# A windowed attention stage: strips issued ahead of stores, its end joined to the next stage, its first two groups' queries set in the stage in front

## What is computed

```python
x = x + 0.5 * _L0_ffn_ref(_layernorm(x, axis=-1), ...)
x = x + _L0_attn_ref(_layernorm(x, axis=-1), ...)
x = x + 0.5 * _L0_ffn_ref(_layernorm(x, axis=-1), ...)
x = x + 0.5 * _L1_ffn_ref(_layernorm(x, axis=-1), ...)
x = x + _L1_attn_ref(_layernorm(x, axis=-1), ...)
x = x + 0.5 * _L1_ffn_ref(_layernorm(x, axis=-1), ...)
```

```python
qkv = (x @ Wqkv.T + bqkv).reshape(B, S, 3, H, d).transpose(2, 0, 3, 1, 4)
...
scores = jnp.einsum('bhncd,bhnld->bhncl', qc, kb) / np.sqrt(d)
...
scores = jnp.where(band, scores, -jnp.inf)
attn = jax.nn.softmax(scores, axis=-1)
o = jnp.einsum('bhncl,bhnld->bhncd', attn, vb).reshape(B, H, S, d)
...
return o @ Wout.T + bout
```

## Time and profile before

| | us |
|---|---|
| median of 3 runs | 1857.52 |
| lowest and highest | 1851.13, 1860.44 |
| the profiled execution | 1860.59 |
| its span, first to last instruction | 1858.4 |

### The profile page before, as it was taken

The page is one execution under the profiler, slowest core; times in us unless marked ns, Lnnn a source line. Parts: engine busy times, 40 slices in busy tenths (PEclk is TensorE's granted clock), DMA queues, the critical chain, the costliest instruction groups (busy, mean ns, idle before and its releaser), DMA issues. The chain is left out here.

```text
span 1858.4 us, 40266 instructions
## 1 busy us (share of the span) xinstructions
PE 1652.9 (89%) x14217; PEld 1417.0 (76%) x14217; DVE 1260.3 (68%) x2948; ACT 1073.2 (58%) x1947; POOL 1196.9 (64%) x1189
## 2 busy tenths in 40 slices
PE   7999898998999989987788999999888788889999
PEld 6888777787878868766567888788767677777887
DVE  2359889888798887988996436443457677646443
ACT  3476766766667766666664544343467566643442
POOL 4238787886878758788896706465655555434663
PEclk9999999999999989999999999999888898889999
DMA  5023333233333323232231501111555556311113
GB/s 151 1 72 117 96 103 111 95 97 98 106 90 120 102 79 110 82 113 87 81 97 29 154 6 48 35 48 43 156 164 148 158 153 177 86 33 38 48 48 106
DMA packets 141088, 171.22 MB, mean 92 GB/s; under 512 B 32246, under 2 KB 76316, under 8 KB 140892
## 3 DMA queue, kind: packets, MB, share of 16 engines
q1 hardware_dynamic: 133852, 153.06, 27.6%
q0 software_dynamic: 7040, 15.60, 2.7%
HBM read 116.30 MB, written 52.30 MB: 91 GB/s over the span
## 5 line engine op out<-in xcount | busy, mean ns | idle before, releaser
L833 POOL TENSOR_TENSOR db<-du_m,bt 128x512 f32<-128x512 f32 x256 | 328.4, 1284 | 115.3 <-DVE bank L838 114.6
L838 DVE TENSOR_TENSOR_SCAN bank<-bank,db 128x512 f32<-128x512 f32 x256 | 312.6, 1221 | 18.3 <-ACT bank L823 17.8
L864 POOL TENSOR_TENSOR y_m<-y_m,ph 128x512 f32<-128x512 f32 x240 | 313.1, 1305 | 2.0 <-DVE ph L853 2.0
L823 ACT ACTIVATE bank<-dt_m,a_neg 128x512 f32<-128x512 f32 x256 | 176.3, 689 | 88.2 <-DVE ph L853 81.2
L853 DVE TENSOR_TENSOR ph<-bank,ct 128x512 f32<-128x512 f32 x240 | 165.9, 691 | 8.4
L1368 POOL TENSOR_TENSOR s_a<-s_a,mx_a 128x768 f32<-128x768 f32 x64 | 94.1, 1471 | 74.4 <-DVE mx_a L1459 73.4
L1445 PE MATMUL bank<-kT_a,qd_a 128*128 128x96 f32 x512 | 79.7, 303 | 34.7 <-ACT qd_a L1269 32.7
L1478 ACT COPY pT_a<-bank 96x512 f32<-96x512 f32 x128 | 68.9, 579 | 66.5 <-PE bank L1471 66.2
L375 PEld LDWEIGHTS bank<-dn,hf2b 128*128 128x128 f32 x680 | 91.7, 197 | 16.0 <-DVE x_all L437 8.3
L1445 PEld LDWEIGHTS bank<-kT_a,qd_a 128*128 128x128 f32 x512 | 70.0, 211 | 42.3 <-ACT qd_a L1269 35.8
L375 PEld LDWEIGHTS bank<-dn,hf1b 128*128 128x128 f32 x680 | 89.1, 192 | 16.0 <-DVE x_all L437 6.8
(11 more groups left out here) (474 smaller groups left out, 4761.1 us busy)
## 6 DMA issues: line engine op xcount, KB each, us to landing
bt<-bc_rows SPq DMA_DIRECT2D x128, 256.0 KB, 3.5
ct<-bc_rows SPq DMA_DIRECT2D x128, 256.0 KB, 3.4
sorted<-zero_row SPq DMA_DIRECT2D x64, 288.0 KB, 3.9
kT_a<-k_rows SPq DMA_DIRECT2D x32, 256.0 KB, 3.5
q_strips_a<-q_rows SPq DMA_DIRECT2D x32, 256.0 KB, 3.9
q_rows<-q_hi_a SPq DMA_DIRECT2D x16, 256.0 KB
q_rows<-q_lo_a SPq DMA_DIRECT2D x16, 256.0 KB
k_rows<-k_hi_a SPq DMA_DIRECT2D x16, 256.0 KB
```

The source lines that it names most:

```text
L823: eng.activation(DH[J % 2][:], dt[s % 2][:, j % NH, :], ACT.Exp, scale=a_neg[:, j % NH, j // NH:j // NH + 1]).then_inc(da_done.sem)
L833: eng.tensor_tensor(db[J % RD][:], du[s % 2][:, j % NH, :], bt[N % RB][:], ALU.mult).then_inc(db_done.sem)
L838: eng.tensor_tensor_scan(DH[J % 2][:], DH[J % 2][:], db[J % RD][:], 0.0, ALU.mult, ALU.add).then_inc(hs_done.sem)
L864: eng.tensor_tensor(y[s % 2][:, j % NH, :], y[s % 2][:, j % NH, :], ph[J % RP][:], ALU.add).then_inc(ys_done.sem)
```

## The change

Seven things are changed.

1. SP's order. The strips of the next sequence's groups 1, 2 and 3 move from k = 3, 5, 6, behind the store of that step, to k = 1, 3, 5 (2, 3, 5 in the first sequence), ahead of it. `load_out` moves ahead of the step's store and of the values' store and loads. In the opening, groups 2 and 3 go ahead of the values.
2. Rings. There are three `q_strips` (RS) and four `kT` (RK) instead of two and three. Some small tiles now share memory so that this fits; the gaps in the layout keep tiles of the two stages apart.
3. Places. TensorE's turned output (`turn_out`) goes ahead of the turns, ScalarE's `copy_out` ahead of `copy_p`. `norm_out` of step 5 goes behind the copies. "T" goes from k = 6, place 0 to place 2. The projection goes from k = 5, place 0 to place 2.
4. The first two groups. Both are cleared and their queries are set in the stage in front: POOL does heads 2 and 3 of both at the end of its list (`set_ahead`), ScalarE heads 0 and 1 of both behind its last gelu.
5. The end. `load_out`, the projection and its addition for the last sequence go into the next stage, through the dictionary `closing`. The 28 warming matmuls are gone.
6. The last norm of the sixth block, for sequence 7, comes later: its mean behind the addition, its root behind the first rows sent, its scale at v = 5.
7. Two tiny activations load the function tables: Exp ahead of the first exponentials, Gelu in step 62.

```diff
@@ attention
-    RQ = 3
+    RQ, RS, RK, HOLE, GAP = 3, 3, 4, UB * KW + 3 * P, 3 * P
...
@@ strips
-            if n >= 2:
-                eng.wait_ge(q_set.sem, q_set.at(n - 2, 1))
-                eng.wait_ge(q_set2.sem, q_set2.at(n - 2, 3))
-            if n >= RQ:
-                eng.wait_ge(sc_done.sem, sc_done.at(2 * (2 * (n - RQ) + 1) + 1))
+            if n >= RS:
+                eng.wait_ge(q_set.sem, q_set.at(n - RS, 1))
+                eng.wait_ge(q_set2.sem, q_set2.at(n - RS, 3))
+            if n >= RK:
+                eng.wait_ge(sc_done.sem, sc_done.at(2 * (2 * (n - RK) + 1) + 1))
...
+        def set_ahead(eng):
+            eng.wait_ge(ob_done.sem, ob_done.at(0))
+            for n in range(2):
+                set_queries(eng, eng.tensor_copy, n, (2, 3))
+                eng.wait_ge(q_set2.sem, q_set2.at(n, 3))
...
@@ sync
-            load_values(eng, 0)
             strips(eng, 0, 2)
             strips(eng, 0, 3)
+            load_values(eng, 0)
...
+                if k == 2 and s >= 1:
+                    load_out(eng, s - 1)
+                if k in ((1, 3, 5) if s >= 1 else (2, 3, 5)) and more:
+                    strips(eng, s + 1, {1: 1, 2: 1, 3: 2, 5: 3}[k])
                 if t >= 2:
                     store_out(eng, t - 2)
                 if k == 2 and more:
                     store_values(eng, s + 1)
                     load_values(eng, s + 1)
-                if k in (3, 5, 6) and more:
-                    strips(eng, s + 1, {3: 1, 5: 2, 6: 3}[k])
-                if k == 2 and s >= 1:
-                    load_out(eng, s - 1)
-            load_out(eng, NSEQ - 1)
@@ pool
-            clear_group(eng, 1)
-            set_queries(eng, eng.tensor_copy, 1, (2, 3))
-            eng.wait_ge(q_set2.sem, q_set2.at(1, 3))
@@ prepared
-            names = ... else {(6, 0): "T", (7, 0): "q", (7, 2): "k", (1, 0): "v"}
+            names = ... else {(6, 2): "T", (7, 0): "q", (7, 2): "k", (1, 0): "v"}
@@ pe of attention
+                if t >= 2:
+                    turn_out(eng, t - 2)
                 for place in range(3):
...
-                    if t >= 2 and place == 2:
-                        turn_out(eng, t - 2)
...
-                    for seq in projected(t) if place == 0 else ():
+                    for seq in projected(t) if place == 2 else ():
                         project_pe(eng, seq)
...
-                if t == NU:
-                    warm(eng, BT[0], K["up_hi"][0], 4)
-            warm(eng, BT[0], K["up_hi"][0], 20)
-            project_pe(eng, NSEQ - 1)
-            warm(eng, BT[0], K["up_hi"][0], 4)
@@ act of attention
             norm_out(eng, 1)
-            set_queries(eng, eng.copy, 1, (0, 1))
+            eng.activation(table[:], C["one"][:], ACT.Exp)
...
-                if k == 5 and s + 2 < NSEQ:
-                    norm_out(eng, s + 2)
+                if t >= 2:
+                    copy_out(eng, t - 2)
...
-                    if place == 2 and t >= 2:
-                        copy_out(eng, t - 2)
+                    if place == 2 and k == 5 and s + 2 < NSEQ:
+                        norm_out(eng, s + 2)
...
                 if t == NU - 2:
+                    eng.activation(table[:], C["one"][:], ACT.Gelu)
                     next(norms_next)
@@ ffn1, pool
+                opening["clear_group"](eng, 1)
                 opening["bias_out"](eng, 0)
+                opening["set_ahead"](eng)
@@ ffn1, pe
+                if v == 1 and closing:
+                    closing["project_pe"](eng, NSEQ - 1, HT[1].psum)
+                    HT[1].free = closing["projected"]
@@ ffn1, act
-                if opening and J >= AJ - 1:
-                    opening["set_queries"](eng, eng.copy, 0, (0, 1))
                 shared_act(eng, J)
...
             if opening:
-                opening["set_queries"](eng, eng.copy, 0, (2, 3))
+                for n in range(2):
+                    opening["set_queries"](eng, eng.copy, n, (0, 1))
@@ ffn1, dve
+                if v == 2 and closing:
+                    closing["project_dve"](eng, NSEQ - 1, HT[1].psum)
+                    eng.wait_ge(*closing["projected"])
+                    norms.mean(eng, NSEQ - 1)
```

84 lines of the change are left out of this document (47 added, 37 removed).

## The result

| | before | after |
|---|---|---|
| median, us | 1857.98 (6 runs) | 1834.95 (6 runs) |
| lowest and highest | 1851.13, 1860.44 | 1832.39, 1844.64 |
| span of the profiled execution | 1858.4 | 1832.1 |

The account below looks back on a forecast made before the run. TensorE bounds the kernel, idling for oT and ScalarE's queries while its clock falls. Opening 4.2, first stretch 1.5, steady periods 25.2, last stretch 8.0 and join 4.0 sum to 42.9 us off 1857.52: 1814.6 us, range 1803 to 1834.

Parts of the forecast that it names:

- The steady periods: Five eight-step attention periods, from scores at k = 5 to the next such: 31.7 us each, 25.2 us saved in all.
- S to K7: From TensorE's scores at k = 5 (S) to those at k = 7 (K7): 8.3 us, ended by ScalarE's cast.
- K7 to S: From TensorE's scores at k = 7 to the next period's at k = 5: not shortened, 22.0 to 23.8, mean 22.9 us.
- Rival (a): Transfers of stores, strips and loads become the bound: a steady period takes 34.1 us, 1828 us in all; chance 0.17.
- (b): ScalarE's xn at k = 5 waits for the values' store; that stretch stays 13.7 us, 1849 us in all; chance 0.09.
- (c): Slower by the clock: TensorE's idling in spread pieces keeps it down, 1870 us at a clock of 0.70; chance 0.06.
- (d): No effect, because other waits covered the wait for oT: 1857 us; chance 0.03.
- The reordering: Steady steps: turned output ahead of the turns, small copy ahead of the large: costed at nothing, possibly 0.2 us a step.
- The last S to K7: Last stretch from scores at k = 5 to k = 7, without xn or turning: 6.3 us instead of 14.3, 8.0 saved.
- The border in front: Stage in front to attention: block ends with the second group's casts, attention begins near 1331.4 instead of 1334.3, 2.9 us saved.
- The opening: Attention's first scores to step 5: 1.3 us saved by earlier strips; step 5 to step 7: 1.5 saved.
- The tail: From the last scores at k = 7 to the next stage: 4.7 us gained, with the table load costing 1.3.

Follow-up runs that it names:

- the last kernel: Changed kernel without POOL's DRAINs at ffn and attention block ends, values' loads a step later, first sequence's strips apart, last addition and mean later: 1826.44 us, 0.9832 of before.

## Why the forecast was right and wrong

**The steady periods: right, in part by luck.** 24.5 of 25.2 us, S to K7 8.2 to 10.1 instead of 8.3, K7 to S 21.9 to 25.8 instead of 22.9. The wait changed its name to ScalarE's cast, and oT was in time. Its load went out at 1437.11, 3.8 us ahead of S; I had said 2. Rival (a), transfers as the bound, did not come in the steady part: a period took 31.8 us, not 34.1. (b) was there in small: 3.4 us for the values' store in three places. (c) and (d) fell, with clock and projection as shown. The reordering was costed at nothing, and one run puts 7 us in five periods on it, all of it between K7 and S (24.9 us a period there, 23.1 in the kernel after). If so, I had the total right and this term wrong. And by the spread of the same code, 157.1 to 164.8 us, the gain could have come out anywhere from 18.8 to 26.5.

**The last S to K7: right**, 7.1 us instead of 6.3.

**The border in front: the step that failed most, 7.8 us.** "The block ends with the second group's casts", I wrote. I read the end of a block from the last instruction that does work, and I took the crossing of 0.7 us, measured behind VectorE, for all of it. What the runs showed in its place: the block ended when POOL's DRAIN was through, 9.3 us behind POOL's last work (1329.67 to 1338.93), in place of 0.7. The row was in the trace of before: POOL's DRAIN, which ended at 1332.7, 1.6 us ahead of the border. I moved work in front of it and counted only the work. I asked what it costs if work loses its cover ("without that cover it would put 2 us on the end of the block"), but of the clearing alone, and it should have been asked of the end of POOL's list. The row of POOL's first work behind the border ("10.63 <-POOLq L2243") looked like idling and was a DRAIN.

**The opening: 5.6 us.** The scores of step 5 came 36.1 us behind the start instead of 34.2, and step 7 12.0 behind those instead of 8.3. The k stores' landing took 4.4 us (3.4 before), group 0's strips about 4.1 (3.1), with group 1's behind them; I had given the earlier strips only a gain. Around the wait of 5.5 us TensorE ran at 1.2 GHz for two steps, which is the other half. Here (a) was right at one place. Why the transfers were late is open. The Trainium skill's DMA: Bandwidth & Descriptors (Queues, rings and completion order) has each DMA engine work through a ring in order; with the strips apart, step 5 stood at 32.6 and 32.4 us in two runs, against 33.4 to 36.6 in nearly all others with the order of the change. That would agree, but one of those others had 30.7. And the strips' time does not follow: with group 1's strips right behind, group 0's took 3.0 to 4.9 us, and with SP's old order, where nothing of the kind stood behind them, 4.4. The k stores, which go out ahead of all strips, took anything from 2.8 to 4.9 us to land. The step behind it gained 1.9 us that I had not counted.

**The tail: 2.1 us, and more in other executions.** The table load cost its 1.3. What I left out is that a store stands behind strips in SP's list too, and that the small copy, now first, asks for its buffer 1.9 us sooner. I looked at what the strips gained by going ahead and not at what went behind them.

**The next stage: 1.4 us more than counted.** The slow start was as forecast: the six matmuls took 0.63 us each (the first 0.77), and the first gelu stood 2.9 us behind the stage's first matmul (3.1 before, where the table load came first, 1.7 with the old end and its warming matmuls). With that, the rule that I cited from the Trainium skill's TensorE: Matmul & The Clock Gate (Part 1: The HAM clock gate) agrees. The addition was given as -1.0 with a bound of -2.2; it stood ahead of xT_lo, cost 1.8 us of wait, and again the clock behind it.

The terms together: 7.8 at the border, 5.6 in the opening, 2.1 in the tail, 1.4 in the next stage and 1.5 in the middle, less the 1.9 us between step 7 and the first S, make up the 16.6 us between 42.9 and 26.3, but for rounding. Each miss that involved the clock has one form: I priced a wait by its length, while TensorE went at half speed behind it.

## What to carry over

Before work is moved to the end of a list, look at what the engine's queue still does behind its last instruction. An idle engine at a block's end may be in its DRAIN, and GpSimd's grew with the indirect DMAs issued since the last one. Measure it from the end of the engine's last work, since its row can begin before that. If each of those DMAs is waited for by its own semaphore, the DRAIN can be left out, as the last kernel does, but at every border up to the end, or the next one pays. And when transfers are moved ahead in a queue, list what now stands behind them and price a new wait of TensorE by the clock it loses, not by its length.

## What the runs showed of the hardware

- GpSimd's DRAIN at a block's end, from the end of GpSimd's last work or from its own start, whichever is later: 0.07 us without indirect DMAs, 0.16 with one, 6.4 with 78, 9.1 with 110 (in every profile that has one), so 0.08 us for each. Its row can begin while that work still runs, and is then up to 2.6 us longer. One that was skipped left its work to the next (9.1 us at a border where it had been 0.07). Behind a DRAIN with nothing issued since, its row was 0.055 us.
- DRAINs between rounds of indirect DMAs made a stage of 242 to 246 us 256 to 263 long.
- The same attention code, in ten executions, took 157.1 to 164.8 us for its five periods and 32.7 to 43.3 for its tail (eight of them), with the tail's granted clock anywhere from 1.00 to 0.72. One profile is not enough to tell 5 us in such a stage.
